# A graph-attention layer on one core: the last blocks of nodes are finished one by one, and the start is staffed otherwise

## The reference

```python
q = x @ wq.T + bq;  k = x @ wk.T + bk;  v = x @ wv.T + bv
q2 = (q @ wiq.T + biq)...;  k2 = (k @ wik.T + bik)...;  v2 = (v @ wiv.T + biv)...
scores = einsum('hnd,hmd->hnm', q2, k2) / 8 + mask      # mask from the edges
out = einsum('hnm,hmd->hnd', softmax(scores), v2)
x = layernorm(x + out @ wo.T + bo)                      # over the 1024 features of a node
```

## Time and profile before

| | |
|---|---|
| median of 3 runs | 285.09 us (285.01 to 286.27) |
| the profiled execution | 285.22 us |
| its span, first to last instruction | 283.5 us |
| PE busy | 274.6 us (97%) |
| DVE, ACT, POOL busy | 179.3, 161.8, 147.5 us |
| mean granted TensorE clock | 0.993 of full speed |

### The profile page before, as it was taken

How to read it: one execution, slowest core, us unless ns; L and a number is a source line. 1 busy time by engine, 2 the same in 40 slices (tenths; PEclk the granted TensorE clock), 3 DMA queues, 4 the chain that set the end, 5 groups by cost and what they waited for, 6 DMA issues and landing times.

```text
span 283.5 us, 4987 instructions
## 1 busy us (share of the span) xinstructions
PE 274.6 (97%) x1578; PEld 248.2 (88%) x1578; DVE 179.3 (63%) x434; ACT 161.8 (57%) x304; POOL 147.5 (52%) x131
## 2 busy tenths in 40 slices
PE   8999999999999999999999999999999999999990
PEld 8999999999999998888999988879797987777880
DVE  5879976576666666323517687867768686701084
ACT  5964234334324424431238899898989898943033
POOL 2000635556635554643886559494755749497000
PEclk9999999999999999999999999999999999999997
DMA  7959866364563436953403869777684958660013
GB/s 263 338 157 347 304 187 217 107 189 148 151 232 137 147 95 239 354 206 115 192 10 140 166 177 213 176 216 138 180 172 143 203 148 205 155 162 2 0 74 148
DMA packets 51920, 49.29 MB, mean 174 GB/s; under 512 B 41056, under 2 KB 41920, under 8 KB 51776
## 3 DMA queue, kind: packets, MB, share of 16 engines
q1 hardware_dynamic: 49792, 47.63, 57.1%
q0 software_dynamic: 1680, 0.62, 0.9%
q10 hardware_dynamic: 432, 0.85, 0.8%
HBM read 37.44 MB, written 2.21 MB: 140 GB/s over the span
## 4 chain that ended last, share of the span: by engine, by line
PE 89%; DVE 6%; ACT 2%; DMA 1%; issue 1%; DVEq 0%; ACTq 0%
PE bank L965 20%; PE bank L956 18%; PE bank L957 17%; PE bank L958 17%; PE bank L1057 7%; PE bank L1039 4%; PE bank L981 3%; DVE stats L930 2%; PE bank L974 1%; DVE res L929 1%; DMA scratch<-shared 1%; ACT shared L541 1%; DVE shared L862 1%; DVE plane_lo_odd L862 1%; ACT h_hi L518 0%
## 5 line engine op out<-in xcount | busy, mean ns | idle before, releaser
L399 POOL DMA_INDIRECT mask_cells<-scratch x48 | 55.5, 1157 | 71.4 <-DMA mask_cells<-scratch 28.9
L458 ACT ACTIVATE w_hi<-w_raw 128x1024 fp32r<-128x1024 f32 x49 | 51.5, 1053 | 22.9 <-PE bank L965 21.1
L956 PE MATMUL bank<-x_hi,w_hi 128*128 128x384 f32 x176 | 58.8, 334 | 0.0
L957 PE MATMUL bank<-x_lo,w_hi 128*128 128x384 f32 x176 | 58.8, 334 | 0.0
L958 PE MATMUL bank<-x_hi,w_lo 128*128 128x384 f32 x176 | 58.8, 334 | 0.0
L354 POOL TENSOR_TENSOR w_lo<-w_raw,w_hi 128x1024 fp32r<-128x1024 f32 x17 | 40.8, 2404 | 30.7 <-DVE plane_lo_odd L862 27.3
L667 DVE TENSOR_TENSOR w_lo<-w_raw,w_hi 128x1024 fp32r<-128x1024 f32 x31 | 37.9, 1226 | 16.9 <-ACT w_hi L458 15.9
L501 ACT ACTIVATE h_hi<-bank,bcol 128x384 f32 (+1 forms) x24 | 13.9, 581 | 54.8 <-PE bank L958 54.7
L956 PE MATMUL bank<-h_hi,w_hi 128*128 128x384 f32 x128 | 44.5, 348 | 0.0
L958 PE MATMUL bank<-h_hi,w_lo 128*128 128x384 f32 x128 | 42.9, 335 | 0.0
L957 PE MATMUL bank<-h_lo,w_hi 128*128 128x384 f32 x128 | 42.8, 334 | 0.0
(11 more groups left out here) (102 smaller groups left out, 459.4 us busy)
## 6 DMA issues: line engine op xcount, KB each, us to landing
w_raw<-weights SPq DMA_DIRECT2D x53, 512.0 KB, 3.8
shared<-key_rows SPq DMA_DIRECT2D x6, 512.0 KB
shared<-start SPq DMA_DIRECT2D x5, 320.0 KB, 5.9
res<-x_rows SPq DMA_DIRECT2D x1, 1536.0 KB, 6.9
out<-res SPq DMA_DIRECT2D x6, 256.0 KB, 2.0
mask_cells<-scratch POOLq DMA_INDIRECT x48
shared<-start ACTq DMA_DIRECT2D x2, 320.0 KB, 5.0
mask_cells<-mask SPq DMA_DIRECT2D x1, 576.0 KB, 6.3
```

The lines of the kernel that those rows point to most:

```text
L399: nc.gpsimd.indirect_dma_start(out=mask_cells, out_offset=bass.IndirectOffsetOnAxis(ap=cell[:, c:c + 1], axis=0), in_=cell_value[:, c:c + ...
L458: nc.scalar.activation(w_part(t, s, slice(0, F))[0], w_raw[:, s, :], ACT.Copy).then_inc(w_hi_done, 1)
L956: pe.matmul(out_ps, w_hi[:, s, cols], moving_hi, start=(k == 0), stop=False)
L957: pe.matmul(out_ps, w_hi[:, s, cols], moving_lo, start=False, stop=False)
```

## The change

At the start, DVE instead of ACT makes the high part of x's block 0, ahead of its other work, with a semaphore of its own (`x_hi_first`); the counts that wait for `x_hi_done` are one lower. `WARM_UP` is 7, not 9. At the end, PE runs k = 4 to 7 of node block 0 in one go, then those of node block 1, then block 2 piece by piece, where each narrow piece runs all its eight k together.

```diff
-WARM_UP = 9
+WARM_UP = 7
...
-                act.wait_ge(start_loaded[k], 16)
-                nc.scalar.activation(x_hi[:, k, :], x_raw(k), ACT.Copy).then_inc(x_hi_done, 1)
+
+                if k:
+                    act.wait_ge(start_loaded[k], 16)
+                    nc.scalar.activation(x_hi[:, k, :], x_raw(k), ACT.Copy).then_inc(x_hi_done, 1)
...
             def start_low(k):
 
+                if k == 0:
+                    dve.wait_ge(start_loaded[0], 16)
+                    nc.vector.tensor_copy(x_hi[:, 0, :], x_raw(0)).then_inc(x_hi_first, 1)
...
-                pe.wait_ge(x_hi_done, k + 1)
+                pe.wait_ge(*((x_hi_done, k) if k else (x_hi_first, 1)))
...
             values(a, 1)
-            for k in range(4, KT - 1):
-                project(0, k)
-                project(1, k)
-
-            pe.wait_ge(sum_done, 2 * a + 1)
-            for k in range(4):
-                project(2, k, slice(1, 3))
-            for ins in project(0, KT - 1):
-                ins.then_inc(y_ready, 1)
-            for ins in project(1, KT - 1):
-                ins.then_inc(y_ready, 1)
+
+            for n in range(NT - 1):
+                for k in range(4, KT):
+                    last = project(n, k)
+                for ins in last:
+                    ins.then_inc(y_ready, 1)
+
+            pe.wait_ge(sum_done, 2 * a + 2)
             for i in range(len(OUT_PIECES[2])):
-                for k in range(4, KT):
+                for k in range(4 if i == 0 else 0, KT):
                     last = project(2, k, slice(i, i + 1))
                 last[0].then_inc(y_ready, 1)
```

More of the change, by code:

```diff
@@ L198, in gnn_layer @@
         biv_loaded, bo_loaded = sem("biv_loaded"), sem("bo_loaded")
-        x_hi_done, x_lo_done = sem("x_hi_done"), sem("x_lo_done")
+        x_hi_first, x_hi_done, x_lo_done = sem("x_hi_first"), sem("x_hi_done"), sem("x_lo_done")
         w_hi_done, w_lo_dve, w_lo_pool = sem("w_hi_done"), sem("w_lo_dve"), sem("w_lo_pool")
@@ L675, in start_low @@
                     .then_inc(*((first_lo, 1) if k < KT - 1 else (w_lo_dve, FIRST_TILES)))
-                dve.wait_ge(x_hi_done, k + 1)
+                dve.wait_ge(*((x_hi_done, k) if k else (x_hi_first, 1)))
                 nc.vector.tensor_tensor(x_lo[:, k, :], x_raw(k), x_hi[:, k, :].bitcast(F32),
```

## The result

The changed kernel took 283.99 us in the median of 5 runs (282.98 to 284.28), the kernel before 285.09 (now also 5 runs, 285.01 to 286.27). The ratio, worked out over rounds of both kernels, is 0.994, 95% interval 0.9917 to 0.9962. Measured a second time it took 283.18 (283.06 to 283.99) against 285.29 for the kernel before beside it, ratio 0.9935 [0.9921, 0.9948]. The gain is real, 1.7 to 1.9 us by the ratios; I had forecast 2.2 and a time of 282.9. The prediction also drew a line at 0.5% (283.66): the first median is above it, and its interval takes the line in; the second lies beyond it with its whole interval.

The account below looks back on a forecast made before the run. Prediction: PE's matmul queue bounds the kernel up to the end, DVE the end behind a late first block. 285.22 - 1.97 - 0.25 + 0.05 = 283.05, 0.13 above the median, so 282.9 us; range 282.3 to 283.9.

Parts of the forecast that it names:

- 282.9: Whole kernel: predicted time against 285.09; the forecast case, 282.5 to 283.3, had chance 0.63.
- DVE bounds the end, behind a late first block: End: DVE gets nothing until 268.94, then finishes three node blocks one behind the other.
- 1.97 us: End: with the new order DVE's last addition starts at 276.12, not 278.09; all that follows is unchanged.
- 0.05 for the tight wait: End, block 0's k = 7: PE now comes at 260.62, close behind POOL's last low parts; 0.05 us lost.
- the rival of a late POOL: Block 0's k = 7: other timing in the softmax before shifts POOL's chain against PE's; 283.4, chance 0.07.
- 0.25 for the start: Start: fewer warm-ups and DVE's copy let PE begin earlier; 0.21 to 0.30 us gained, 0.25 taken.
- no more than 0.5 can be had: Start: block 1 sets the floor, as ACT gets its data at 5.36 and finishes `x_hi` at 6.19.
- more than that: Start: the clock in most executions rises later than 6.35, so the shorter warm-up gives 0.4; 282.6, chance 0.05.
- The clock rival: Start: the hole before the first product holds the clock down through blocks 1 and 2; 1.8 us, 284.7, chance 0.07.
- my middle of 0.48: Start: DVE's copy of 384 columns, taken midway between bounds of 0.40 and 0.56 us.
- only the end counts: Start gives nothing or takes up to 0.5, by later clock rise or slow DVE copy; 283.2 to 283.7, chance 0.15.
- Both signs that I had named for being wrong: PE's last matmul starting later than 275.8, or matmul spacing staying at 0.32 beyond 6.4.

Follow-up runs that it names:

- the mixed one: Kernel before with the new order of the last products and seven warm-up products, ACT making the first high part of x as before: 283.30 us, ratio 0.9935.
- the late GpSimd: Changed kernel with one more unread 128 x 384 subtraction on GpSimd ahead of the attention's last low part: 284.10 us, ratio 0.9967.
- The end alone: Kernel before with only the new order of the last products; nine warm-ups and ACT's first high part of x kept: 283.23 us, ratio 0.9935.

## Why the prediction was right or wrong

- **DVE bounds the end, behind a late first block: right.** With the new end the stretch from tile 2 on is 267.51 or 267.52 under the old start, the new one and the mixed one; with the old end it is 269.46 or 269.47 under either start.
- **1.97 us: right**, 1.94 measured. PE's last product starts 261.81 behind tile 2, before it 261.77; DVE's last addition 0.31 behind that (I took 0.33). Block 1's first addition comes at 268.18 and block 0's at 262.74, each within 0.05 of the forecast once the later start is taken off.
- **0.05 for the tight wait: 0 measured**, and the cover is about 0.1 us thin, as the late GpSimd showed. Without it the loss is whole, as forecast. In no trace without the added subtraction does PE wait for GpSimd there, so the rival of a late POOL didn't happen.
- **0.25 for the start: not borne out as worked out.** The weak step is the end of block 0: 0.21 to 0.30 means that its six products end at 6.44 to 6.53 and not at 6.74. What leads up to it held (the copy took 0.36, the pair started at 4.55, and in the second trace block 0 was through at 6.43). The first pair of the kernel before starts at 4.99 in its trace and not at the 5.14 that I worked out (5.78 less two products of 0.32), but the 0.15 between the two stands in the changed kernel's too (4.55 to 5.33, 0.14 more than 0.64), so that drops out. The 0.32 itself is what a product of 384 columns takes ahead of the rise: in the changed kernel's second trace pairs start at 5.15, 5.79 and 6.43. But I took from one trace both the rise of the clock at 6.35 (6.36 by the trace's record) and with it 6.74 as what the kernel before does. It does so only where the clock rises that late; in its second trace block 1 starts at 6.38, bound by ACT, and there the changed start has nothing to gain. I had this floor in the prediction, as "no more than 0.5 can be had", but put it 0.1 too low, since from ACT's end to PE's first product go 0.14 to 0.15 and not 0.05: 0.4 could be had in the first trace. A rise later than 6.35 stands in 2 of the 13 traces (6.36 and 6.83), so the rival "more than that", which needs it in most executions, has little left, and the worked-out gain is one of a rare case. No run shows the 0.25: by time the start's value stays open, between the 0.27 and 0.05 of the medians side by side and a ratio of 1.0003 that spans 0.4 gained to 0.6 lost.
- **The clock rival** named a cost that no trace shows; that a hole ahead of the first product holds the clock down was an assumption of mine. With seven warm-ups the clock rises between 4.27 and 6.83, with nine between 3.98 and 6.36, by where each trace's record of the granted clock begins, at full speed; these ranges overlap, so a small effect of the hole can't be told, but the spacing of 0.32 through blocks 1 and 2 that the rival needs is in none of them. The end alone idles for 0.50 at block 1, behind its rise, and its pairs go on at 0.51 to 0.59. In the changed kernel's second trace the pair at 5.15 takes 0.84 and those from 7.01 on 0.51, with the rise at 6.83 between them. DVE's copy of 384 columns took 0.36 in every trace that has it; my middle of 0.48 was 0.12 too long, and it made no difference.
- **282.9** was 1.1 below the first median and 0.3 below the second. The repeat's 283.18 lies inside the forecast's 282.5 to 283.3 and at the edge of the rival "only the end counts", 283.2 to 283.7, so the times don't tell the two apart; the first median lies 0.1 beyond the whole range, and that a repeat came inside is partly the luck of which executions had a late block. Both signs that I had named for being wrong came true in one trace each: PE's last product at 276.56, not 275.8, in the first, from the late block, and a spacing of 0.32 beyond 6.4 in the second, from the late clock. The missing term for the scatter is the landing of the first blocks, which no part of my range had: 1.0 us in one execution of the changed kernel. Whether the executions above 284 all had a late block can't be told, as only one of them has a trace.

## What to carry to other kernels

Where several results are finished one behind the other by a second engine, order the products so that each result is complete as early as it can be: nothing was saved on TensorE here, and 1.9 us came from starting VectorE's 3.5 us per block while TensorE still worked. It holds only while the last inputs come in time: GpSimd had 0.1 us to spare. A gain at the start is worth only what the next producer allows: find what the second step waits for, in more than one execution, before counting what the first step saves. And divide a trace at a point that all changes leave alone: with the same end the rest repeated within 0.02 us (267.51 to 267.52, 269.46 to 269.47), where the totals scattered by 1; the traces show the difference in the start.

## What the runs showed of the hardware that I had not expected

- The record of TensorE's granted clock begins, at full speed, at 3.98 us after the span's start in one execution and at 6.83 in another, of nearly the same program, and between the two in the other eleven; pairs of products of 384 columns take 0.84 before and 0.51 behind (5.15 and 7.01 in the second of these), though TensorE always began at 1.13 or 1.14.
- The same 320 KB block, issued at 1.28 on SP's queue, was there for ACT between 5.36 and 5.58 in nine traces and once at 6.39. With a third load on ACT's queue that one landed at 8.81; with all blocks on one queue, in order, block 1 was there at 4.75 and 4.84.
- A product of 128 columns with weights of its own costs 0.111 us (22 intervals in 2.45), against 0.120 for 256 columns.
